# A two-layer graph network on one core: the layer between, the scores of the second layer and its ring of gathered rows

## The reference, cut to what matters

```python
x = _layernorm(x + _L0_gnn_ref(...), axis=-1)
# _L1_gnn_ref(x, edge_index, edge_weight, W, a_src, a_dst):
h = jnp.einsum('ni,hio->hno', x, W)
attn_src = jnp.einsum('hno,hod->hn', h, a_src)
attn_dst = jnp.einsum('hno,hod->hn', h, a_dst)
e = attn_src[:, src_idx] + attn_dst[:, dst_idx]
e = jnp.where(e >= 0, e, NEG_SLOPE * e)
e = e * edge_weight[None, :]
e_exp = jnp.exp(e - jnp.max(e))
denom = jax.ops.segment_sum(e_exp.T, dst_idx, num_segments=num_nodes).T
alpha = e_exp / (denom[:, dst_idx] + 1e-10)
msg = h[:, src_idx] * alpha[..., None]
# out = segment_sum of msg over dst, then
x = _layernorm(x + out, axis=-1)
# _layernorm(x): (x - mean) / sqrt(var + 1e-5)
```

## Time and profile before

| | |
|---|---|
| Median of three runs | 2341.45 us (2336.84 to 2349.82) |
| Profiled execution, its own time | 2339.09 us |
| Its span | 2337.0 us |
| Busy: TensorE, VectorE, ScalarE, GpSimd | 1864.5, 1558.8, 1312.5, 1563.2 us |
| Stage between the layers | 1590 to 1641 us |
| Second layer | 1641 to 2281 us |

### The profile page before, as it was taken

The page is one execution under the profiler, slowest core; times in us unless marked ns, Lnnn a source line. Parts: engine busy times, 40 slices in busy tenths (PEclk is TensorE's granted clock), DMA queues, the critical chain, the costliest instruction groups (busy, mean ns, idle before and its releaser), DMA issues. The chain is left out here.

```text
span 2337.0 us, 37065 instructions
## 1 busy us (share of the span) xinstructions
PE 1864.5 (80%) x11350; PEld 1657.2 (71%) x11350; DVE 1558.8 (67%) x4222; ACT 1312.5 (56%) x2397; POOL 1563.2 (67%) x1253
## 2 busy tenths in 40 slices
PE   7799999999999999999999999976234455554550
PEld 7688888888888888888888888865224444444440
DVE  6556666666666666666666666645357788788786
ACT  2477777777777777777777777744112222222232
POOL 0417787777777777777877777752756667766714
PEclk9899999999999999999999999987555555555555
DMA  7788887777877777777777777765434445544523
GB/s 248 264 228 185 189 173 165 163 165 165 168 165 165 165 160 160 162 159 162 164 160 165 178 176 175 161 120 175 128 98 124 130 131 139 139 131 128 137 63 113
DMA packets 239702, 370.84 MB, mean 159 GB/s; under 512 B 33255, under 2 KB 172481, under 8 KB 239495
## 3 DMA queue, kind: packets, MB, share of 16 engines
q0 software_dynamic: 104688, 191.38, 41.8%
q1 hardware_dynamic: 134807, 177.00, 25.2%
HBM read 260.28 MB, written 107.97 MB: 158 GB/s over the span
## 5 line engine op out<-in xcount | busy, mean ns | idle before, releaser
L1570 POOL DMA_INDIRECT accA<-ystage,to_a x391 | 648.1, 1657 | 198.4 <-issue 103.6
L1576 POOL DMA_INDIRECT GA<-TA,src_c x391 | 432.9, 1107 | 247.9 <-issue 105.7
L1627 POOL DMA_INDIRECT Hg<-HT,src_c x391 | 411.0, 1051 | 182.7 <-issue 116.0
L646 DVE TENSOR_TENSOR h2l<-h2f,h2h 128x512 fp32r<-128x512 f32 (+1 forms) x294 | 203.0, 691 | 311.7 <-ACT h2h L2018 155.1
L1946 PE MATMUL bank<-xb_hi,in_window 128*128 128x260 f32 x391 | 177.7, 454 | 239.7 <-issue 239.7
L1702 PE MATMUL bank<-h1h,W1h 128*128 128x512 f32 x882 | 354.0, 401 | 8.7 <-DVE h1l L646 8.7
L2055 ACT ACTIVATE h1f<-bank 128x512 f32<-128x512 f32 (+1 forms) x392 | 220.9, 591 | 232.6 <-PE bank L1757 186.3
L1703 PE MATMUL bank<-h1l,W1h 128*128 128x512 f32 x882 | 348.7, 395 | 0.0
L1704 PE MATMUL bank<-h1h,W1l 128*128 128x512 f32 x882 | 348.6, 395 | 0.0
L2018 ACT ACTIVATE xb_hi<-xb 128x1024 fp32r<-128x1024 f32 (+1 forms) x99 | 103.3, 1044 | 377.1 <-DVE xb L1120 213.7
L1946 PEld LDWEIGHTS bank<-xb_hi,in_window 128*128 128x128 f32 x391 | 128.0, 327 | 243.0 <-issue 243.0
(11 more groups left out here) (256 smaller groups left out, 4744.5 us busy)
## 6 DMA issues: line engine op xcount, KB each, us to landing
ef<-in_eT SPq DMA_DIRECT2D x97, 256.0 KB
bcast_i<-in_src_row SPq DMA_DIRECT2D x97, 256.0 KB
TW<-TB SPq DMA_DIRECT2D x116, 203.0 KB
HB<-hist SPq DMA_DIRECT2D x98, 130.0 KB
rel<-RL SPq DMA_DIRECT2D x97, 128.0 KB
rem<-RD SPq DMA_DIRECT2D x48, 256.0 KB
TB<-stB SPq DMA_DIRECT2D x24, 406.0 KB
accA<-zeros SPq DMA_DIRECT2D x4, 2193.0 KB, 15.6
```

Source lines behind the costliest of these rows:

```text
L646: return dve.tensor_tensor(o, full, hi.bitcast(f32), ALU.subtract)
L1570: return pool.indirect_dma_start(out=table, out_offset=bass.IndirectOffsetOnAxis(ap=rows, axis=0), in_=sums, in_offset=None, compute_op=AL ...
L1576: pool.indirect_dma_start(out=GA[0:n, b % (GAR * BLOCKS_PER_GROUP), :].bitcast(f32), out_offset=None, in_=TA, in_offset=bass.IndirectOffse ...
L1627: pool.indirect_dma_start(out=Hg[0:n, slot, :], out_offset=None, in_=HT, in_offset=bass.IndirectOffsetOnAxis(ap=src_c[0:n, b:b + 1], axis= ...
```

## The change

It has three parts.

**Products of rows that are not normalised.** TensorE transposes and multiplies the rows of `xn` as they are after the residual (it waits for `s_res` in place of `s_x1`), with a `Wc` from whose rows the mean over the 256 inputs has been taken off: TensorE sums the columns of `Wc` with a matrix of ones (`sums_p`, two matmuls after the twenty of the identity), and VectorE subtracts 1/256 of the sum, between its first and its second chunk. The product is scaled by `rstd` in the copy to `hst`. ScalarE writes the normalised rows, needed only in the last stage, after all products. The product ring has 6 banks (it had 4), the transposes 2 (they had 4), and the copy to `hst` comes five tiles behind the transposes, not two. `Wc` is loaded after the first chunk's tables, not after the third's.

**Destination scores five pairs ahead.** `one_hot` and `destination_scores` run five pairs ahead (they were three), SyncE's loads for them seven (they were five). ScalarE copies each pair's scores from `PAD` to a ring `ad_s` of eight pairs in SBUF (`keep_scores`, a new instruction, ahead of `upper_rows(2q)`), `edge_scores` reads them there, and TensorE waits for that copy before it overwrites `PAD`. `window_scores` comes one iteration earlier. `ad_s` and `xb` lie inside the tile `fin`, which the last stage uses.

**Ring of 12 groups.** `Hg` has 12 groups in place of 10.

```diff
-        HGR = 10
+        HGR = 12
+        AHEAD, ADSR = 5, 8
+        HR = 6
+        sums_p = bank[3][:, P:P + OUT + 2 * HEADS]
             for c in range(NC):
                 mean_residual(c)
+                if c == 0:
+                    dve.wait_ge(s_wa, 2)
+                    for k in range(DK):
+                        last = dve.scalar_tensor_tensor(Wc[:, k, :], sums_p, -1.0 / D, Wc[:, k, :], ALU.mult, ALU.add)
+                    last.then_inc(s_wac, 1)
...
-                dve.wait_ge(s_ad, q + 1)
+                dve.wait_ge(s_adc, q + 1)
...
-                            PAD[0:n, j * ADP:(j + k) * ADP].rearrange("p (k c) -> p k c", c=ADP)[:, :, part * HEADS:(part + 1) * HEADS],
+                            ad_s[0:n, q % ADSR, j * ADP:(j + k) * ADP].rearrange("p (k c) -> p k c", c=ADP)[:, :, part * HEADS:(part + 1) * HEADS],
...
-            for q in range(-3, NQ + 1):
+            for q in range(-AHEAD, NQ + 1):
...
-                if q + 3 < NQ:
-                    one_hot(q + 3)
+                if q + AHEAD < NQ:
+                    one_hot(q + AHEAD)
...
-                if q >= 0 and 2 * q % ADC == 2 and 2 * q // ADC + 1 < NG // ADC:
+                if q >= 0 and 2 * q % ADC == 0 and 2 * q // ADC + 1 < NG // ADC:
                     window_scores(2 * q // ADC + 1)
...
-            load_tables(sp, range(TSR))
-            sp.dma_start(Wc[:, :, 0:OUT], Wcat.rearrange("(k p) n -> p k n", p=P)).then_inc(s_ldWc, 16)
-            load_tables(sp, range(TSR, 5))
+            load_tables(sp, range(1))
+            sp.dma_start(Wc[:, :, 0:OUT], Wcat.rearrange("(k p) n -> p k n", p=P)).then_inc(s_ldc, 16)
+            load_tables(sp, range(1, 5))
...
-                pe.wait_ge(s_x1, t + 1)
-                if t >= 4:
-                    pe.wait_ge(s_x1c, t - 3)
+                pe.wait_ge(s_res, t + 1)
+                if t >= 2:
+                    pe.wait_ge(s_x1c, t - 1)
...
+            pe.wait_ge(s_wac, 1)
+            pe.wait_ge(s_ldc, 16 * (2 + 2 * HEADS))
+            for k in range(DK):
+                last = pe.matmul(sums_p, ones[:, :], Wc[:, k, :], start=k == 0, stop=k == DK - 1)
+            last.then_inc(s_wa, 1)
...
-            copy(hst[0:n, t % 4, :], bank[t % 4][0:n, 0:BW + HEADS]).then_inc(s_hc, 1)
+            act.wait_ge(s_rstd, [t in tiles for tiles in CHUNKS].index(True) + 1)
+            act.activation(hst[0:n, t % 4, :], bank[t % HR][0:n, 0:BW + HEADS], ACT.Copy,
+                           scale=rstd[0:n, t:t + 1]).then_inc(s_hc, 1)
...
-            deviations(0, 0)
             for t in range(NT):
-                for c, tiles in enumerate(CHUNKS):
-                    if t == tiles[0]:
-                        normalise(c, c)
-                    if t == tiles[2 * len(tiles) // 3] and c + 1 < NC:
-                        deviations(c + 1, c + 1)
...
+                for c, tiles in enumerate(CHUNKS):
+                    if t == tiles[-1]:
+                        deviations(c, c)
+                if t >= HR - 1:
+                    rows_copy(act, t - HR + 1)
+            for t in range(NT - HR + 1, NT):
+                rows_copy(act, t)
+            for c in range(NC):
+                normalise(c, c)
...
+            def keep_scores(q):
+                act.wait_ge(s_ad, q + 1)
+                if q >= ADSR:
+                    act.wait_ge(s_sc, SCS * (q - ADSR) + 2)
+                blocks = blocks_of_window_pair(q)
+                for run in same_rows(blocks):
+                    n, v = rows_of_block(run[0]), slice((run[0] - blocks[0]) * ADP, (run[-1] + 1 - blocks[0]) * ADP)
+                    last = copy(ad_s[0:n, q % ADSR, v], PAD[0:n, v])
+                last.then_inc(s_adc, 1)
+
+            for q in range(AHEAD - 2):
+                keep_scores(q)
             exponentials(0)
             for q in range(NQ):
+                if q + AHEAD - 2 < NQ:
+                    keep_scores(q + AHEAD - 2)
                 upper_rows(2 * q)
```

More of the change, by code:

```diff
@@ L1499, in load_remainders @@
                 sp.dma_start(rem[:, q % 2, 0:n], RD[0, a:a + n].partition_broadcast(P)).then_inc(s_rem[q % 2], 16)
-            for q in range(-5, NQ):
-                if q + 5 < NQ:
-                    load_remainders(q + 5)
+            for q in range(-AHEAD - 2, NQ):
+                if q + AHEAD + 2 < NQ:
+                    load_remainders(q + AHEAD + 2)
                 if q >= 0:
@@ L1897, in node_products @@
                 if t == 0:
-                    pe.wait_ge(s_wac, 1)
-                    pe.wait_ge(s_ldWc, 16)
-                if t >= 4:
-                    pe.wait_ge(s_hc, t - 3)
+                    pe.wait_ge(s_wac, 2)
+                if t >= HR:
+                    pe.wait_ge(s_hc, t - HR + 1)
                 for k in range(DK):
-                    last = pe.matmul(bank[t % 4][0:n, 0:OUT + 2 * HEADS], x1T[:, t % XTR, k, 0:n], Wc[:, k, :],
+                    last = pe.matmul(bank[t % HR][0:n, 0:OUT + 2 * HEADS], x1T[:, t % XTR, k, 0:n], Wc[:, k, :],
                                      start=k == 0, stop=k == DK - 1)
@@ L1952, in _ @@
             pe.wait_ge(s_x1c, NT)
-            for q in range(-3, NQ):
+            for q in range(-AHEAD, NQ):
                 if q >= 0:
@@ L2003, in _, with rows_copy @@
                               start=True, stop=True).then_inc(s_vpe, 1)
-        def rows_copy(act, copy, t):
+        def rows_copy(act, t):
             n = rows_of_tile(t)
```

21 lines of the change are left out of this document (10 added, 11 removed).

## The result

The changed kernel takes 2364.23 us in the median of nine runs (2348.53 to 2367.74), the kernel before 2345.97 us beside it (2336.84 to 2349.82). The ratio is 1.0064 with an interval of 1.0041 to 1.0087: slower by 0.6%, where 2334 was forecast. The medians are 18.3 us apart, the ratio stands for 15 us.

A forecast was written before the change was run, and what follows sets the result against it. VectorE was the largest named part, with handovers between engines and waits for TensorE's late results. Gains of 4.4 + 3 = 7.4 us off 2339.09 give 2331.7, or 2334 for the median; 8 in 10 range 2303 to 2357.

The forecast's parts named there:

- Between the layers: Stage between the layers: last copy to `hst` ends near 1634.2 instead of 1638.6, 4.4 us gained, bounds 0 to 9.5.
- VectorE's stop: Between VectorE's first two chunks: it waits for the `Wc` corrections until 1601.6 or 1601.7, so its chain starts 5.1 us late.
- the 6.08 us: Stage between the layers: VectorE's time for a chunk of five tiles, taken as the new pace, above ScalarE's 4.18 us.
- hidden behind the gathers: Start of the second layer: ScalarE's 12.8 us of normalised rows fit behind the first pair's gathers, 10 us or more.
- Scores: Second layer, scores five pairs ahead: the 37.2 us of score waits mostly move to the next sums; 3 us gained, bounds 0 and 37.2.
- The ring: Second layer, 12 groups: GpSimd is already ahead of VectorE and only gets further ahead; counted as 0 us.
- the sum of 7.4 us: Whole kernel: 4.4 us from the stage between the layers plus 3 us from the scores, taken off the time.
- rival two: Second layer: the deeper ring lengthens TensorE's stalls, the first by 10.3 us; 2360 us in all, chance 0.19 for several stalls.
- the coincidence of 1713.2 and 1714.73: Second layer: GpSimd's first unbroken run of gathers ends 1.5 us before VectorE's longest wait, 20.06 us, ends.
- Its second term: Later stalls of the second layer: 5.2 us more each in two or three of ten, 13 us together.
- Its test: First odd group's sum: its wait should end 10 us later behind the first gather than the 73.6 us before the change.

## Why the prediction was wrong, step by step

**Between the layers: right in size, in part by luck.** From the first addition on the tables to the end of the last copy, the old form takes 45.7 to 48.1 us in its five traces, the new one 43.3 to 44.2 us in its fifteen. That is 3.2 us in the mean, where 4.4 was predicted; of the two pairs of traces taken side by side without late results, one has 4.4 us and the other 2.5. The steps were off both ways. VectorE's last statistics come 4.4 us later behind its first addition than before (5.1 forecast), and what stands behind them takes 4.4 us (2.4 forecast), where it had taken 11.9 us. VectorE's stop, TensorE's identity and sums, and the last copies in the changed kernel:

```profile
1595.24 6.58 PE L1920 MATMUL bank<-ident 128*128 128x128 f32 x40 [16.09 <-DMA tab<-accA]
1601.66 1.06 PE L1924 MATMUL bank<-Wc,ones 128*128 128x264 f32 x4
```

```profile
1595.32 0.97 DVE L982 TENSOR_TENSOR tab<-tab 128x774 f32<-128x774 f32 x1 [4.44 <-DMA tab<-accA]
...
1602.75 0.77 DVE L1041 SCALAR_TENSOR_TENSOR Wc<-bank,Wc 128x264 f32<-128x264 f32 x2 [3.53 <-PE bank L1924]
```

```profile
1637.00 1.05 ACT L2028 ACTIVATE hst<-bank,rstd 128x264 f32<-128x264 f32 x2 [0.58 <-PE bank L1913]
1638.37 0.47 ACT L2028 ACTIVATE hst<-bank,rstd 53x264 f32<-53x264 f32 x1 [0.33 <-POOL node L1646]
1638.75 12.37 ACT L2190 ACTIVATE xn<-xn,shift,rstd 128x256 f32<-128x256 f32 x25
1651.03 0.20 ACT L2035 ACTIVATE fin<-bank 128x64 f32<-128x64 f32 x1
```

VectorE stopped for 3.53 us, and with the two corrections its second chunk began 3.5 us later behind the first than before, not 5.1. The pitch was 6.8 us a chunk, not 6.08: in each chunk VectorE waits 0.62 us for ScalarE's root, which stands behind the copy of the chunk's last tile. In the kernel before it had waited for it too, from the third chunk on, at a pitch of 6.74 us; the 6.08 us were those of the chunk ahead of that. A copy with a scale takes 0.47 us, not 0.38. The last copy ended at 1638.84 and not near 1634, for the most part because this execution began the stage 3.35 us later (first addition at 1595.32, before at 1591.97). The normalised rows took 12.37 us and held ScalarE's first copy of scores to 1651.03. They were hidden behind the gathers, as I had said: VectorE's first scores waited for a gather until 1654.49, 12.3 us behind the first gather, where it had been 12.0 us.

**Scores: right in the mechanism.** The waits for scores went and came back at the sums: 37.2 us left, and ring 10 with the change has 130.5 us of waits in all against 122.6. I counted 3 us of gain; alone it measured 1.0004. That the waits would move was right; the 3 us are not shown. A small cost that I counted at nothing is there too. An undisturbed pair takes 9.38 us in the traces with the scores ahead and 9.30 us in those without, as in the earlier trace rows. The additions take 0.18 to 0.19 us as before; it is `diag`, the multiplication of the identity with the maximum, that takes 0.35 us instead of 0.29. Why is not shown. In 49 pairs this is at most 3.9 us, as much as the stage between the layers gains. By the Trainium skill, page "SBUF — State Buffer", section "Who interferes with whom", a VectorE instruction with two SBUF sources contends with a GpSimd instruction that reads SBUF, so the two additions could have held GpSimd. The traces show nothing of it: on the chip without late results the 391 gathers take 529.4 us with them and 531.4 without.

**The ring: this is the step that failed.** "A deeper ring lets it be further ahead, and I count 0" put a term at nothing for no other reason than that GpSimd is ahead of VectorE anyway. Measured, it is 19 us between rings of 12 and 10 in the changed kernel (12 to 27 by the intervals). With it the sum of 7.4 us gained becomes a loss of 11.6 us. The mechanism of rival two is what the runs support: GpSimd gathers longer without a stop, TensorE's results are late in such a stretch, and the first stall grows. It had a chance of 0.19, and I had set the coincidence of 1713.2 and 1714.73 aside as one that could run the other way. Rival two's size for the first stall, 10.3 us, fits the 10.4 and 11.8 us of the two pairs. Its second term does not: 13 us in the later stalls were named, and none were found. So that its total, 19 us above the median of then, comes near the measured 18.3 us is in part luck. Its test, the end of the 20 us wait against the first gather, would have misled: 78.1 against 73.6 us, with a ring of 12 alone even 71.5, for that wait is 20.0 to 20.1 us long with a ring of 10 or 12. The growth sits in the wait behind it. And that results come at GpSimd's stop is too simple: in the changed kernel the 20 us wait ended 3.7 us before the stop, and with the ring of 12 alone 11.3 us before it.

**Open.** What inside the chip holds TensorE's results back while GpSimd issues gathers, and why only some series have it. Where the rest of the 19 us goes beyond the 10 us in the first stall. Why the ring alone costs 0.1% (up to 0.3% in its interval) in the kernel before and 0.8% beside the other parts. The traces do not show this difference: from the last copy to `hst` to the last `scale` the second layer is 14.6 us longer with the ring alone (657.3 against 642.7 us) and 15.3 us in the changed kernel (665.7 against 650.4 us). But the first profile of the kernel before is of an execution of 2339.09 us, 7 us below its median, and one execution of each can't settle it.

## What to carry to other kernels

When a wait has no named releaser and the result it waits for is recorded as finished long before, look at what the other engines were doing until it came, before pricing any wait as fixed; and ask of each buffer that is made deeper which engine will now run longer without a stop. A coincidence of two times is tested by moving one of them: here one number, the depth of the ring, would have done it. Measure a change of less than 1% on more than one chip where such waits appear, and time the old kernel against itself beside it: the same change was slower by 0.6% in one series, and in another 0.15% ahead where the old kernel stood at 0.07% against itself.

## What the runs showed of the hardware that I had not expected

- The same kernel differs by up to 6% between series: it took 2346, 2348, 2347 and 2373 us in four series and 2239, 2247 and 2246 us in three others. The difference is in the second layer (642.7 against 559.8 us for the kernel before, 665.7 against 558.5 us for the changed one), where in some series VectorE waits up to 20.1 us, and once 27.2 us, for TensorE's results in long runs of gathers.
- Late results come in bunches: four updates of TensorE within 0.23 us at 1805.14. In the changed kernel with ring 8, 10 or 12 VectorE has 26 waits of 5 us and more behind the first stall. They end 31 to 50 us after GpSimd had last resumed, eight of them at 39.7 to 40.0 us. In the place shown, the last update for a sum ahead of the stall is recorded at 1788.94, 23.6 us into the run and 5.5 us behind the recorded end of that sum.
- A quarter of the gathered rows changes a gather of GpSimd from 1.05 to 1.00 us on average, so its price is nearly the same for 32 and for 128 rows here.
